# Chains of VectorE issued in turns, and two products moved ahead, in a gated attention and expert kernel

## The chip, the cores and the metric

One core of a Trainium2 chip runs the kernel. The metric is device time in microseconds. The kernel before takes 648.89 us (median of three runs, 648.76 to 652.68). The engines have their own queues and meet through semaphores: TensorE (PE, with its weight loads PEld), VectorE (DVE), ScalarE (ACT), GpSimd (POOL) and SyncE (SP), which issues transfers. An engine works through its queue in order: an instruction that waits holds up all that stand behind it.

## The reference

The input has 32 sequences of 128 tokens and 256 features. A gated attention over a context of the same shape comes first, then a layer of eight experts of which each token takes two.

```python
ig = (gi @ igate_w.T + igate_b).transpose(0, 2, 1)       # gi = [q, k, v], q = layernorm(x), k = v = ctx
fg = (gi @ fgate_w.T + fgate_b).transpose(0, 2, 1)
cs = jnp.cumsum(jax.nn.log_sigmoid(fg), axis=-1)
log_D = where(tril, cs[..., :, None] - cs[..., None, :], -inf) + ig[..., None, :]
max_log_D = jnp.max(log_D, axis=-1, keepdims=True)
C = (einsum('bhsd,bhtd->bhst', qh, kh) / sqrt(dh)) * jnp.exp(log_D - max_log_D)
normalizer = jnp.maximum(jnp.abs(C.sum(-1, keepdims=True)), jnp.exp(-max_log_D))
h = jnp.einsum('bhst,bhtd->bhsd', C / (normalizer + EPS), vh)
x = x + layernorm_per_head(h) * out_w                     # x1
xf = layernorm(x); scores = softmax(xf @ gate_w); two best experts per token
x = x + sum over the two of score * (gelu(xf @ w1[e] + b1[e]) @ w2[e] + b2[e])
```

## The kernel before

The kernel has two stages. The first goes through the sequences in eight steps of four (S0 to S7). It also loads the experts' weights and splits them into a high and a low half. The second goes through tiles of up to 256 rows that belong to one expert each.

The first stage is software-pipelined. After a prologue there are five bodies, and each works on four steps at once: `after` is the next x to come (its layer norm, its turn to features by tokens, its gates), `nxt` has its decays and its first two products made, `step` has its last two products made and its heads finished (normalizer, variance, scaling, `out_w`, x1), and `last` is routed (x1's norm `xf`, logits, choice of two experts, rows to the expert table). The last body has no `after`. The order on each engine is written out by hand in the four functions `body(last, step, nxt, after)`.

The pieces that the steps below speak of, with their lines before the change:

- VectorE: `c_of` (L1749) multiplies scores by decays, the product c of one sequence j = 0 to 3. `next_stats` (L1637 to 1643) and `next_norm` (L1631 to 1656) make the scale and shift of the next x, the last of it `minus_mean_rstd`. `next_a` (L1687, 1690) makes the gate columns, `running_max` (L1699, 1700) their running maximum, `split` three bf16 parts of it, `max_log_decay` (L1727) a sum with the turned maximum. `weights_low` (L1740) is a "weights rest", of which a body has four. `h_norm` (L1759 to 1769) makes the variance of the heads, `h_scaled` and `h_weighted` (L1780, 1785) scale them. `choose` (L1817 to 1832) is the choice of experts, eleven small instructions, and `records` what is written of it. `Chain.link` lets an instruction signal a semaphore and the next wait for it, since the next reads what it wrote.
- ScalarE: `next_guess`, `h_guess`, `x1_guess` (L720, 721) are two table lookups each that give a first guess of a reciprocal root, which Newton's step on VectorE refines. `next_normed` (L732) normalizes a sequence of the next x, `turned` (L750) copies its turn out of PSUM, `q_low` what is left, `x1_normed` (L742) makes a row block of xf, `xf_turned` and `xf_low` (L828, 760) copy its turn, `weights_high` (L801) the weights' high half, `h_out` (L809, 810) copies a sequence's heads, `decay` (L789) takes the exponential.
- TensorE: `turn` (L1142, 1145) turns a sequence of the next x, `turn_a` (L1201) the gate columns, `turn_max` (L1207) the maximum. `times_v` (L1278) multiplies c by v. `logits` (L1304), `ranks` and `decay_args` speak for themselves. `stream` (L1228) are products that nothing reads. The first `turn` of a body also waits for the fourth product, whose scores lay in the same PSUM banks.

Of the kernel before, what the change touches and what calls it, by code (L numbers as in the profile page):

```python
# [5 lines left out]
ALU = mybir.AluOpType  # L6
# [7 lines left out]
P = 128  # L14
# [33 lines left out]
def build(nc, x, ctx_in, igate_w, igate_b, fgate_w, fgate_b, out_w, gate_w, w1, b1, w2, b2, out):  # L48
# [51 lines left out]
    with ExitStack() as ctx:  # L100
# [320 lines left out]
        with nc.Block() as block:  # L421
# [287 lines left out]
            def _(act):  # L709
# [136 lines left out]
                def body(last, step, nxt, after):  # L846
                    if last is not None:
                        x1_normed(last, 0)
                        x1_normed(last, 1)
# [13 lines left out]
                    if step is not None:  # L863
                        h_out(step, 2)
# [8 lines left out]
                    if last is not None:  # L873
                        x1_normed(last, 3)
                    if step is not None:
                        h_out(step, 3)
                    if after is not None:
                        q_low(after, 0)
# [248 lines left out]
            def _(pe):  # L1127
# [205 lines left out]
                def body(last, step, nxt, after):  # L1333
                    if step is not None:
                        scores(step, 3)
                    if last is not None:
                        turn_xf(last, 0)
                    if nxt is not None:
                        log_f_sum(nxt)
                    if step is not None:  # L1340
                        stream_before(step, 2, 3)
                        times_v(step, 2)
                    if last is not None:
                        xf_left(last, 0)
# [6 lines left out]
                    if step is not None:  # L1351
                        times_v(step, 3)
# [274 lines left out]
            def _(dve):  # L1627
                dve.wait_ge(s_cp, 21)
                def refine(c, var, y, t):

                    c.link(dve, dve.tensor_tensor(t, y, y, ALU.mult))  # L1631
                    c.link(dve, dve.scalar_tensor_tensor(out=t, in0=t, scalar=-0.5, in1=var, op0=ALU.mult, op1=ALU.mult))
                    c.link(dve, dve.scalar_tensor_tensor(out=y, in0=t, scalar=1.5, in1=y, op0=ALU.add, op1=ALU.mult))

                def stats(c, src, parts, mean_var, var_eps, ready):
                    for j in range(SB):
                        c.inc(dve.bn_stats(parts[:, j, :], src[:, j, :]))  # L1637
                    c.wait(dve)
                    dve.sem_inc(s_held, 1)
                    for j in range(SB):  # L1640
                        c.inc(dve.bn_aggr(mean_var[:, j, :], parts[:, j, :]))
                    c.wait(dve)
                    dve.tensor_scalar(var_eps[:, :], mean_var[:, :, 1], LN_EPS, None, ALU.add).then_inc(ready, 1)

                def next_stats(step):
                    c_dn.begin(number(step))
                    dve.wait_ge(s_x, (number(step) + 1) * 16)
                    stats(c_dn, xin[:, :, :], st, mv, ve, s_ve)
                    c_dn.end(8)

                def next_norm(step):
# [3 lines left out]
                    refine(c_dn, ve[:, :], rs[:, :], nt1[:, :])  # L1655
# [4 lines left out]
                def gate_bias(step):  # L1660
# [5 lines left out]
                    c_dg.link(dve, dve.scalar_tensor_tensor(  # L1666
                        out=gs[:, :, :, :].rearrange("p j a h -> p j (a h)"),
                        in0=ps_gate.rearrange("p j a h -> p j (a h)"), scalar=1.0 / W_SCALE, in1=bias,
                        op0=ALU.mult, op1=ALU.add))
                    dve.scalar_tensor_tensor(out=nabs[:, :, :], in0=f, scalar=-1.0, in1=f, op0=ALU.mult,  # L1670
# [10 lines left out]
                def next_a(step):  # L1681
# [5 lines left out]
                    c_dg.inc(dve.tensor_copy(csb[:, :], ps_cs))  # L1687
                    gates_i = gs[:, :, 0, :].unsqueeze(1).broadcast_to([P, 3, SB, NH])
# [14 lines left out]
                def split(step):  # L1703
# [8 lines left out]
                    c.link(dve, dve.tensor_copy(to, runs[:, :, :]))  # L1712
                    left = runs[0:2 * G, :, :]
                    c.link(dve, dve.tensor_tensor(left, left, to[0:2 * G, :, :], ALU.subtract))
                    c.link(dve, dve.tensor_copy(to[0:2 * G, :, :], left))
# [36 lines left out]
                def h_norm(step):  # L1752
# [4 lines left out]
                    dve.wait_ge(s_en, g + 1)  # L1757
                    sq = work[:, :, :].rearrange("p j (h e) -> p (j h) e", h=NH)
                    c.inc(dve.tensor_reduce(ssq[:, :], sq, AX, ALU.add))  # L1759
                    rows = Hs[:, :, :, DH]  # L1760
                    c.link(dve, dve.scalar_tensor_tensor(out=nrm[:, :, :], in0=rows, scalar=-1.0, in1=rows,
                                                         op0=ALU.mult, op1=ALU.max))
                    c.link(dve, dve.scalar_tensor_tensor(out=nrm[:, :, :], in0=en[:, step[1], :, :], scalar=HUGE,
                                                         in1=nrm[:, :, :], op0=ALU.min, op1=ALU.max))
                    n = nrm[:, :, :].rearrange("p j h -> p (j h)")
                    c.link(dve, dve.tensor_scalar(n, n, EPS, None, ALU.add))
                    c.link(dve, dve.scalar_tensor_tensor(out=hv[:, :], in0=n, scalar=LN_EPS, in1=n,
                                                         op0=ALU.mult, op1=ALU.mult))
# [4 lines left out]
                def h_scaled(step):  # L1773
# [4 lines left out]
                    refine(c, hv[:, :], hy[:, :], ht[:, :])  # L1778
# [15 lines left out]
                def x1_stats(step):  # L1794
# [3 lines left out]
                    stats(c, xres[:, :, :], st2, mv2, ve2, s_ve2)  # L1798
# [13 lines left out]
                def choose(step):  # L1812
# [4 lines left out]
                    c.link(dve, dve.tensor_reduce(m1[:, :], ps_log, AX, ALU.max))  # L1817
                    c.link(dve, dve.tensor_tensor(dl[:, :, :], ps_log, wide(m1[:, :]), ALU.subtract))
                    c.link(dve, dve.scalar_tensor_tensor(out=key[:, :, :], in0=dl[:, :, :], scalar=0.0,
# [412 lines left out]
```

## Time and profile before

| | |
|---|---|
| runs | 648.76, 648.89, 652.68 us; median 648.89 |
| the profiled execution | 651.1 us, of which the span from first to last instruction is 649.1 |
| mean granted clock of TensorE | 0.986 of 2.4 GHz |
| busy over the span | PE 611.4 us (94%), PEld 526.6, DVE 487.2 (75%), ACT 323.4 (50%), POOL 193.7 (30%) |
| first to last third product of the bodies | 104.2 to 213.75 us |
| the expert stage's first layer-1 product | 247.73 us |

A row of the timeline gives the start in us from the span's start, the duration, engine, line, operation, output and inputs, the count, and in brackets how long the engine stood before it and for whom. The difference of two starts on one engine is what the first costs there; durations are longer than that where the next instruction starts before the first has left the pipe.

### The profile page before, as it was taken

The page shows a single profiled execution, that of the slowest core. Times are in us where ns is not written, and L with a number is a line of the kernel's source. Part 1 is how long each engine was busy: PE and PEld are TensorE (multiplying, and loading weights), DVE is VectorE, ACT ScalarE, POOL GpSimd, SP SyncE. Part 2 cuts the span into 40 slices and gives each one's busy share as a digit, 9 for nine tenths or more (in the row PEclk, how much of TensorE's full clock was granted, in tenths as well). Part 3 has the DMA queues.
Part 4 walks back from the last instruction along what each step waited for, and adds up shares of the span by engine and source line. Part 5 has one row for each costly group of instructions (what it writes and reads, how often), then busy time and mean ns, then how long its engine had stood idle before and what let it go on. Part 6 is the DMA issues. An engine that isn't in the chain of part 4 may idle for free. (4 is left out here: it accounts for less than half of the span.)

```text
span 649.1 us, 20273 instructions
## 1 busy us (share of the span) xinstructions
PE 611.4 (94%) x6736; PEld 526.6 (81%) x6737; DVE 487.2 (75%) x1330; ACT 323.4 (50%) x767; POOL 193.7 (30%) x185
## 2 busy tenths in 40 slices
PE   1799999999999899999999999999999999999995
PEld 1567777777777668998988988888989888989994
DVE  2546988999999898995888967666676757575684
ACT  2677888897988747544432323233232323232341
POOL 3000002242433424235345523232222323232333
PEclk9898998999999999999999999999999999999998
DMA  4443635475655626233464432323132323243510
GB/s 143 134 127 118 209 99 187 147 238 194 220 166 142 198 91 231 70 73 92 75 186 108 70 68 38 65 36 65 33 62 33 66 33 66 67 119 81 141 34 2
DMA packets 56044, 70.22 MB, mean 108 GB/s; under 512 B 5584, under 2 KB 50832, under 8 KB 55840
## 3 DMA queue, kind: packets, MB, share of 16 engines
q1 hardware_dynamic: 42560, 51.80, 26.3%
q0 software_dynamic: 13296, 17.32, 14.7%
q8 instruction: 49, 0.80, 0.5%
q14 instruction: 27, 0.22, 0.1%
q10 hardware_dynamic: 112, 0.08, 0.0%
HBM read 41.50 MB, written 24.92 MB: 102 GB/s over the span
## 5 line engine op out<-in xcount | busy, mean ns | idle before, releaser
L1059 ACT ACTIVATE decay_slots<-scores,b_turned 128x256 f32<-128x256 f32 (+1 forms) x312 | 124.4, 451 | 241.2 <-PE scores L1545 235.1
L1545 PE MATMUL scores<-x_slots,w_halves 128*128 128x256 f16 (+1 forms) x1760 | 193.7, 266 | 0.0
L1545 PEld LDWEIGHTS scores<-x_slots,w_halves 128*128 x1760 | 165.2, 98 | 17.3
L662 POOL DMA_INDIRECT expert_rows<-xf_rows,slot_i x64 | 71.9, 1124 | 211.8 <-issue 107.0
L1559 PE MATMUL pv<-w_halves,decay_slots 128*128 x864 | 97.6, 273 | 0.0
L684 POOL DMA_INDIRECT out_rows<-v_centred_and_one,row_ids x36 | 58.3, 1619 | 129.2 <-DVE v_centred_and_one L2146 95.7
L1559 PE MATMUL gate_bank<-w_halves,q_and_k_halves 128*128 x840 | 95.0, 273 | 0.0
L1559 PEld LDWEIGHTS pv<-w_halves,decay_slots 128*128 128x128 f16 x864 | 84.4, 98 | 9.7
L1559 PEld LDWEIGHTS gate_bank<-w_halves,q_and_k_halves 128*128 128x128 f16 x840 | 82.0, 98 | 9.5
L684 POOL DMA_INDIRECT out_rows<-work,row_ids x35 | 56.2, 1605 | 104.6 <-DVE work L2146 82.6
L1278 PEld LDWEIGHTS pv<-v_centred_and_one,decay_slots 128*128 128x128 f32 x512 | 63.7, 194 | 1.6
L1278 PE MATMUL pv<-v_centred_and_one,decay_slots 128*128 128x33 f32 x512 | 63.8, 260 | 0.0
L2133 DVE TENSOR_TENSOR decay_slots<-decay_slots 128x512 f16<-128x512 f32 (+1 forms) x80 | 51.2, 640 | 2.8
L2133 DVE TENSOR_TENSOR q_and_k_halves<-decay_slots,q_and_k_halves 128x512 f16<-128x512 f32 (+1 forms) x76 | 49.5, 651 | 2.6
L1740 DVE SCALAR_TENSOR_TENSOR w_halves<-weight_stage,w_halves 128x1024 f16<-128x1024 f32 x32 | 38.9, 1219 | 10.7 <-ACT w_halves L801 10.7
L789 ACT ACTIVATE decay_slots<-turn_bank 128x512 f32<-128x512 f32 x64 | 38.3, 598 | 8.6 <-PE turn_bank L1174 8.4
L1749 DVE SCALAR_TENSOR_TENSOR decay_slots<-scores,decay_slots 128x1024 f32<-128x1024 f32 x32 | 39.1, 1221 | 2.0 <-PE scores L1221 2.0
L2122 DVE CAST x_slots<-turn_bank 128x512 f16<-128x512 f32 (+1 forms) x39 | 25.1, 643 | 18.6 <-PE scores L1545 15.9
L1276 PE MATMUL pv<-minus_big_above,ident_bf 128*128 128x240 bf16 x128 | 34.8, 272 | 2.8 <-ACT work L810 1.7
L801 ACT ACTIVATE w_halves<-weight_stage 128x1024 f16<-128x1024 f32 x32 | 33.8, 1057 | 3.4 <-DMA weight_stage<-in_L_ffn_w 3.4
L2131 DVE CAST decay_slots<-decay_slots 128x512 f16<-128x512 f32 (+1 forms) x80 | 33.3, 416 | 2.0 <-ACT decay_slots L1059 2.0
L2131 DVE CAST q_and_k_halves<-decay_slots 128x512 f16<-128x512 f32 (+1 forms) x76 | 32.2, 423 | 0.1
(263 smaller groups left out, 864.5 us busy)
## 6 DMA issues: line engine op xcount, KB each, us to landing
weight_stage<-in_L_ffn_w SPq DMA_DIRECT2D x32, 512.0 KB, 4.0
x_slots<-in_x SPq DMA_DIRECT2D x16, 512.0 KB, 4.4
weight_stage<-expert_rows SPq DMA_DIRECT2D x30, 272.0 KB, 3.2
ctx_slots<-in_ctx SPq DMA_DIRECT2D x8, 512.0 KB, 6.0
out_rows<-x_slots SPq DMA_DIRECT2D x8, 512.0 KB
v_centred_and_one<-expert_rows SPq DMA_DIRECT2D x9, 272.0 KB, 3.0
expert_rows<-v_centred_and_one SPq DMA_DIRECT2D x9, 272.0 KB, 3.2
xf_rows<-w_halves SPq DMA_DIRECT2D x4, 512.0 KB, 4.1
```

The lines of the kernel that those rows point to most:

```text
L662: pool.indirect_dma_start(table, bass.IndirectOffsetOnAxis(ap=sloti[:, step[1], j, k:k + 1], axis=0), xfn[:, step[1], j, :], None, bounds_ ...
L684: pool.indirect_dma_start(out_rows, bass.IndirectOffsetOnAxis(ap=ids[:, k, b:b + 1], axis=0), yo[k][:, b, :], None, bounds_check=T - 1, oo ...
L789: act.activation(E[:, j, HG * r:HG * r + HG, :].rearrange("p c s -> p (c s)"), ps_t[:, :], ACT.Exp).then_inc(s_ee, 1)
L1059: ins = act.activation(hf[:, f * R:f * R + tr.rows(0)], ps_s[:, q, n * R:n * R + tr.rows(0)], ACT.Gelu, bias=b1T[:, bass.ds(expert, 1), f] ...
L1276: pe.matmul(ps_h[:, P + P + 16:512], ident_h[:, :], never[:, 0:120].unsqueeze(1).broadcast_to([P, 2, 120]), start=True, stop=True)
L1278: ins = pe.matmul(ps_h[:, h * (DH + 1):(h + 1) * (DH + 1)], E[:, j, k * KC + u, :], vaug[:, step[1], j, h, :], start=True, stop=True)
L1545: ins = pe.matmul(o, w, xh[:, tr.slot(0) % 2, b, k, 0:tr.rows(0)], start=(n == 0), stop=(n == 3 * KC - 1))
L1559: ins = pe.matmul(ps_y[k % 2][:, c * D:(c + 1) * D], hh[k % 2][:, a, f, c * P:(c + 1) * P], w, start=(f == 0 and n == 0 and c == 0), stop= ...
L1740: dve.scalar_tensor_tensor(out=lo, in0=stage[:, half, :], scalar=W_SCALE, in1=hi, op0=ALU.mult, op1=ALU.subtract).then_inc(s_lo, 1)
L1749: dve.scalar_tensor_tensor(out=c, in0=ps_s[:, :, 0:KC * P], scalar=QK_SCALE, in1=c, op0=ALU.mult, op1=ALU.mult).then_inc(s_cm, 1)
L2131: dve.tensor_copy(hi, src).then_inc(s_hhi, 1)
L2133: dve.tensor_tensor(lo, src, hi, ALU.subtract).then_inc(s_hh, 1)
```

## The change

All of VectorE's chains become generators. Where `link` signalled and waited at once, an instruction now signals, the generator yields, and the wait stands behind the yield. `go_on(chain)` issues one more piece of a chain; `whole(chain)` issues all that is left, and is used where nothing is interleaved (the prologue and the expert stage, whose order stays). The bodies' order is new on three engines. On VectorE, chains alternate, and the fourth product, the gate columns and a weights rest come ahead of the next x's scale. On ScalarE the x1 rows come behind the first h and decay and earlier than the next x's guess, and the fourth h comes ahead of the third normalization. On TensorE the fourth times-V stands ahead of the next x's first turn, and three fillers have become one ahead of the third and one ahead of the fourth times-V.

```diff
 ScalarE
-                    if last is not None:
-                        x1_normed(last, 0)
-                        x1_normed(last, 1)
                     if step is not None:
                         h_out(step, 1)
                         decay(step, 3, 1)
                     if last is not None:
+                        x1_normed(last, 0)
+                        x1_normed(last, 1)
+                    if nxt is not None:
+                        weights_high(nxt, 1)
+                    if last is not None:
                         x1_normed(last, 2)
-                        xf_turned(last, 0)
+                    if step is not None:
+                        h_out(step, 2)
                     if after is not None:
                         next_guess(after)
-                    if nxt is not None:
-                        weights_high(nxt, 1)
+                    if last is not None:
+                        xf_turned(last, 0)
+                        x1_normed(last, 3)
                     if after is not None:
                         next_normed(after, 0)
                         next_normed(after, 1)
                     if step is not None:
-                        h_out(step, 2)
+                        h_out(step, 3)
...
 TensorE
                         scores(step, 3)
+                    if nxt is not None:
+                        log_f_sum(nxt)
+                    if step is not None:
+                        stream_before(step, 2, 1)
+                        times_v(step, 2)
                     if last is not None:
                         turn_xf(last, 0)
-                    if nxt is not None:
-                        log_f_sum(nxt)
                     if step is not None:
-                        stream_before(step, 2, 3)
-                        times_v(step, 2)
+                        stream_before(step, 3, 1)
+                        times_v(step, 3)
...
 VectorE
+                def go_on(chain):
+                    next(chain, None)
+                def whole(chain):
+                    for _ in chain:
+                        pass
                 def refine(c, var, y, t):
-                    c.link(dve, dve.tensor_tensor(t, y, y, ALU.mult))
+                    c.inc(dve.tensor_tensor(t, y, y, ALU.mult))
+                    yield
+                    c.wait(dve)
...
+                    if step is not None:
+                        c_of(step, 2)
                     if last is not None:
                         x1_norm(last)
-                    if step is not None:
-                        c_of(step, 2)
-                    if after is not None:
-                        next_stats(after)
-                    if nxt is not None:
-                        weights_low(nxt, 0)
-                    if after is not None:
-                        next_norm(after)
+                    for _ in range(SB):
+                        go_on(incoming)
                     if step is not None:
                         c_of(step, 3)
-                    if nxt is not None:
-                        next_a(nxt)
+                    go_on(incoming)
+                    go_on(incoming)
+                    if nxt is not None:
+                        weights_low(nxt, 0)
+                    go_on(scaling)
+                    go_on(sums)
...
```

VectorE from the fourth product's neighbourhood to the running maximum. `bn_parts`, `mean_var`, `newton`, `rstd` and `minus_mean_rstd` belong to the next x, `log_f_sum` and `i_minus_sum` are the gate columns, L1749 and L1775 the product, L1740 and L1766 a weights rest. Before:

```order
L1641 BN_AGGR mean_var<-bn_parts 128x2 x4
L1643 TENSOR_SCALAR var_eps<-mean_var 128x4
L1740 SCALAR_TENSOR_TENSOR w_halves<-weight_stage,w_halves 128x1024
L1631 TENSOR_TENSOR newton<-rstd 128x4
L1632 SCALAR_TENSOR_TENSOR newton<-newton,var_eps 128x4
L1633 SCALAR_TENSOR_TENSOR rstd<-newton,rstd 128x4
L1656 SCALAR_TENSOR_TENSOR minus_mean_rstd<-mean_var,rstd 128x4
L1749 SCALAR_TENSOR_TENSOR decay_slots<-scores,decay_slots 128x1024
L1687 COPY log_f_sum<-gate_bank 128x32
L1690 TENSOR_TENSOR i_minus_sum<-gates,gate_bank 128x96
L1740 SCALAR_TENSOR_TENSOR w_halves<-weight_stage,w_halves 128x1024
L1699 COPY a_and_running_max<-gate_bank 96x128
```

And now:

```order
L1775 SCALAR_TENSOR_TENSOR decay_slots<-scores,decay_slots 128x1024
L1657 BN_AGGR mean_var<-bn_parts 128x2 x4
L1660 TENSOR_SCALAR var_eps<-mean_var 128x4
L1766 SCALAR_TENSOR_TENSOR w_halves<-weight_stage,w_halves 128x1024
L1640 TENSOR_TENSOR newton<-rstd 128x4
L1706 COPY log_f_sum<-gate_bank 128x32
L1643 SCALAR_TENSOR_TENSOR newton<-newton,var_eps 128x4
L1710 TENSOR_TENSOR i_minus_sum<-gates,gate_bank 128x96
L1646 SCALAR_TENSOR_TENSOR rstd<-newton,rstd 128x4
L1766 SCALAR_TENSOR_TENSOR w_halves<-weight_stage,w_halves 128x1024
L1673 SCALAR_TENSOR_TENSOR minus_mean_rstd<-mean_var,rstd 128x4
L1719 COPY a_and_running_max<-gate_bank 96x128
```

The fourth product, the gate columns and the second weights rest stood between the scale and the running maximum; now all three stand ahead of the scale, and the running maximum follows it at once.

VectorE from the sum with the turned maximum (`max_log_d`) to the scaling of the heads. `square_sum`, `normalizer` and `h_var` lead to the heads' variance, `h_newton` and `h_rstd` refine its root, `top`, `routing_work`, `xf_rows` and `chosen` are the choice. Before:

```order
L1727 TENSOR_TENSOR max_log_d<-log_f_sum,gate_bank 128x32
L1759 TENSOR_REDUCE square_sum<-work 128x32
L1761 SCALAR_TENSOR_TENSOR normalizer<-h_slots 128x32
L1763 SCALAR_TENSOR_TENSOR normalizer<-exp_minus_max,normalizer 128x32
L1766 TENSOR_SCALAR normalizer<-normalizer 128x32
L1767 SCALAR_TENSOR_TENSOR h_var<-normalizer 128x32
L1769 SCALAR_TENSOR_TENSOR h_var<-square_sum,h_var 128x32
L1740 SCALAR_TENSOR_TENSOR w_halves<-weight_stage,w_halves 128x1024
L1631 TENSOR_TENSOR h_newton<-h_rstd 128x32
L1632 SCALAR_TENSOR_TENSOR h_newton<-h_newton,h_var 128x32
L1633 SCALAR_TENSOR_TENSOR h_rstd<-h_newton,h_rstd 128x32
L1780 TENSOR_TENSOR work<-h_slots,h_rstd 128x1024
```

And now:

```order
L1753 TENSOR_TENSOR max_log_d<-log_f_sum,gate_bank 128x32
L1801 TENSOR_REDUCE square_sum<-work 128x32
L1766 SCALAR_TENSOR_TENSOR w_halves<-weight_stage,w_halves 128x1024
L1804 SCALAR_TENSOR_TENSOR h_var<-square_sum,h_var 128x32
L1852 TENSOR_REDUCE top<-route_bank 128x4
L1855 TENSOR_TENSOR routing_work<-route_bank,top 128x32
L1640 TENSOR_TENSOR h_newton<-h_rstd 128x32
L1858 SCALAR_TENSOR_TENSOR routing_work<-routing_work,rev_index 128x32
L1643 SCALAR_TENSOR_TENSOR h_newton<-h_newton,h_var 128x32
L1863 TENSOR_REDUCE xf_rows<-routing_work 128x4
L1646 SCALAR_TENSOR_TENSOR h_rstd<-h_newton,h_rstd 128x32
L1866 TENSOR_TENSOR chosen<-routing_work,xf_rows 128x32
```

The normalizer has gone up between the pieces of the split. The variance's last instruction stands behind the weights rest, and the choice, which stood behind scaling and weighting, starts ahead of the first of Newton's steps.

## Rows read from the trace of the kernel before

**Rows 1.** The page's 40 slices of the span: TensorE's busy tenths.
```profile
PE   1799999999999899999999999999999999999995
```

**Rows 2.** Stretches between third products: us, busy us by engine, clock, DMA.
```profile
core 0: us, PE busy (x) PEld busy (x) DVE busy (x) ACT busy (x) POOL busy (x), PEclk, DMA share, GB/s
104.20:131.56 27.36, 26.15 (x356) 21.67 (x345) 24.08 (x73) 22.22 (x53) 7.90 (x9) 0.94 0.62 198
158.96:186.36 27.40, 25.88 (x376) 20.97 (x376) 25.74 (x77) 23.56 (x56) 9.45 (x9) 1.00 0.64 198
213.75:243.79 30.04, 27.73 (x358) 19.90 (x356) 27.28 (x85) 16.72 (x40) 10.38 (x9) 1.00 0.50 150
```

**Rows 3.** VectorE's timeline, one body, from its third product to the next.
```profile
158.96 1.23 DVE L1749 SCALAR_TENSOR_TENSOR decay_slots<-scores,decay_slots 128x1024 f32<-128x1024 f32 x1
160.10 1.40 DVE L1637 BATCH_NORM_STATS2 bn_parts<-x_slots 128x6 f32<-128x256 f32 x4
...
163.27 0.16 DVE L1631 TENSOR_TENSOR newton<-rstd 128x4 f32<-128x4 f32 x1
...
163.85 0.16 DVE L1656 SCALAR_TENSOR_TENSOR minus_mean_rstd<-mean_var,rstd 128x4 f32<-128x4 f32 x1
163.93 1.23 DVE L1749 SCALAR_TENSOR_TENSOR decay_slots<-scores,decay_slots 128x1024 f32<-128x1024 f32 x1
...
165.33 1.22 DVE L1740 SCALAR_TENSOR_TENSOR w_halves<-weight_stage,w_halves 128x1024 f16<-128x1024 f32 x1
166.47 0.28 DVE L1699 COPY a_and_running_max<-gate_bank 96x128 f32<-96x128 f32 x1
...
171.24 0.19 DVE L1769 SCALAR_TENSOR_TENSOR h_var<-square_sum,h_var 128x32 f32<-128x32 f32 x1
...
175.56 0.18 DVE L1817 TENSOR_REDUCE top<-route_bank 128x4 f32<-128x32 f32 x1
175.78 0.19 DVE L1818 TENSOR_TENSOR routing_work<-route_bank,top 128x32 f32<-128x32 f32 x1
...
177.79 0.19 DVE L1832 TENSOR_TENSOR chosen<-routing_work,key_max 128x32 bf16<-128x32 f32 x1
177.91 0.22 DVE L1666 SCALAR_TENSOR_TENSOR gates<-gate_bank,gate_bias_rows 128x64 f32<-128x64 f32 x1
...
186.36 1.23 DVE L1749 SCALAR_TENSOR_TENSOR decay_slots<-scores,decay_slots 128x1024 f32<-128x1024 f32 x1
```

**Rows 4.** ScalarE's timeline in the same body.
```profile
157.66 0.21 ACT L720 ACTIVATE ln_var_x<-var_eps_x 128x4 f32<-128x4 f32 x1 [0.41 <-DVE var_eps_x L1643]
...
162.26 0.20 ACT L720 ACTIVATE ln_var<-var_eps 128x4 f32<-128x4 f32 x1
...
164.05 1.09 ACT L732 ACTIVATE x_slots<-x_slots,minus_mean_rstd,rstd 128x256 f32<-128x256 f32 x2 [0.41 <-DVE minus_mean_rstd L1656]
...
167.04 1.08 ACT L750 ACTIVATE q_and_k_halves<-scores 128x512 f16<-128x512 f32 x2
...
169.97 1.10 ACT L801 ACTIVATE w_halves<-weight_stage 128x1024 f16<-128x1024 f32 x1
...
171.87 0.29 ACT L720 ACTIVATE square_sum<-h_var 128x32 f32<-128x32 f32 x1
...
173.29 0.60 ACT L760 ACTIVATE xf_halves_turned<-route_bank 128x512 f16<-128x512 f32 x1
```

**Rows 5.** TensorE's timeline in the same body.
```profile
165.30 0.41 PE L1142 MATMUL scores<-ident,x_slots 128*128 128x128 f32 x2 [1.05 <-DVE decay_slots L1749]
...
165.77 0.27 PE L1201 MATMUL gate_bank<-ident,i_minus_sum 128*96 128x128 f32 x1
...
174.08 0.75 PE L1304 MATMUL route_bank<-router_w_halves,xf_halves_turned 128*128 128x8 f16 x24
```

**Rows 6.** TensorE's timeline where the expert stage begins.
```profile
247.26 0.63 PE L1525 MATMUL turn_bank<-ident,weight_stage 128*128 128x128 f32 x4
```

**Rows 7.** TensorE's timeline in the first body.
```profile
109.05 0.66 PE L1142 MATMUL scores<-ident,x_slots 128*128 128x128 f32 x2 [1.21 <-DMA ctx_slots<-in_ctx]
```

**Rows 8.** A stretch around that wait; columns as in rows 2.
```profile
108.85:112.25 3.40, 3.20 (x17) 3.15 (x17) 3.01 (x8) 3.37 (x8) 1.09 (x2) 0.50 0.62 157
```

More of the change, by code:

```diff
@@ L1832, in choose @@
+                    yield
+                    c.wait(dve)
                     dve.tensor_tensor(chosen[:, 1, :, :], key[:, :, :], wide(kmax[:, :]), ALU.is_equal).then_inc(s_mk, 1)
@@ L1916, in body @@
                 def body(last, step, nxt, after):
+                    nothing = iter(())
+                    incoming, scaling = (next_stats(after), next_norm(after)) if after is not None else (nothing,) * 2
+                    sums, bias = (next_a(nxt) if nxt is not None else nothing,
+                                  gate_bias(after) if after is not None else nothing)
+                    parted = split(nxt) if nxt is not None else nothing
+                    norm, scaled = (h_norm(step), h_scaled(step)) if step is not None else (nothing,) * 2
@@ L1917, in body @@
+                    choice, record = (choose(last), records(last)) if last is not None else (nothing,) * 2
+                    outgoing = x1_stats(step) if step is not None else nothing
+                    if step is not None:
+                        c_of(step, 2)
                     if last is not None:
                         x1_norm(last)
+                    for _ in range(SB):
+                        go_on(incoming)
                     if step is not None:
-                        c_of(step, 2)
@@ L1929, in body @@
+                    go_on(scaling)
+                    go_on(sums)
+                    go_on(scaling)
                     if nxt is not None:
-                        next_a(nxt)
                         weights_low(nxt, 1)
+                    go_on(scaling)
+                    if nxt is not None:
                         running_max(nxt)
-                        split(nxt)
+                    go_on(parted)
+                    go_on(norm)
+                    go_on(parted)
+                    go_on(norm)
@@ L1934, in body @@
+                    go_on(parted)
+                    go_on(norm)
+                    go_on(parted)
+                    go_on(norm)
+                    if nxt is not None:
                         max_log_decay(nxt)
-                    if step is not None:
-                        h_norm(step)
+                    go_on(norm)
                     if nxt is not None:
                         weights_low(nxt, 2)
+                    go_on(norm)
+                    go_on(choice)
+                    go_on(choice)
@@ L1939, in body @@
+                    go_on(scaled)
+                    go_on(choice)
+                    go_on(scaled)
+                    go_on(choice)
+                    go_on(scaled)
+                    go_on(choice)
+                    go_on(scaled)
+                    go_on(choice)
                     if step is not None:
-                        h_scaled(step)
                         h_weighted(step)
-                    if last is not None:
-                        choose(last)
-                    if after is not None:
-                        gate_bias(after)
+                    go_on(choice)
@@ L1958, in body @@
                         c_of(nxt, 2)
-                    if step is not None:
-                        x1_stats(step)
-                    if last is not None:
-                        records(last)
+                    go_on(outgoing)
+                    go_on(record)
+                    go_on(outgoing)
+                    go_on(record)
+                    go_on(outgoing)
+                    go_on(record)
+                    go_on(outgoing)
+                    go_on(record)
+                    go_on(outgoing)
+                    go_on(outgoing)
                 def first_steps():
-                    next_stats(S0)
-                    next_norm(S0)
+                    whole(next_stats(S0))
+                    whole(next_norm(S0))
                     weights_low(S0, 0)
@@ L2027, in first_steps @@
                     log_f(S3)
-                    records(S0)
+                    whole(records(S0))
                 first_steps()
```

194 lines of the change are left out of this document (120 added, 74 removed).

## The prediction

> **What bounds the kernel now.** I read the busy shares in slices first, then the stretches of single bodies, then VectorE's, ScalarE's and TensorE's timelines in one of them. After the first third of the span TensorE is full in every slice [rows 1]: the expert stage follows at its own pace, and a microsecond won or lost in the bodies ahead of it moves the end by one. The reader should see in the stretches [rows 2] that a body takes 27.40 us from one third product to the next, that TensorE is busy for 25.88 of it and VectorE's sum is 25.74; and on VectorE's timeline [rows 3] that its instructions touch one another over the whole body. So VectorE sets the 27.40. Its small instructions show two prices: a choice that needs the one in front starts 0.22 after it (175.56 to 175.78), and one that needs nothing starts 0.11 to 0.12 after it (177.79 to 177.91). That difference is what the change is after.
>
> **What it saves.** I count, in the old order, 27 places where a small instruction waits for the one in front and now has another chain's between them: 3 in Newton's steps of the next x, 3 in the split, 4 in the normalizer, 4 in the heads' scaling, 9 in the choice, 1 in the gates, 3 in the records. 27 x 0.115 = 3.1 us. The x's statistics wait some 0.2 before their sums, and the fourth product now fills that. The heads' row sum and the running maximum's column sum lose short old waits, some 0.6. Together about 3.9 us a body.
>
> **What it moves, and what then waits.** I follow one body from the third product's start, old times by [rows 3 to 5] less 158.96.
>
> First, the next x's scale (`minus_mean_rstd`). Old: 4.89 (163.85), ahead of the fourth product. Now ahead of it stand the third product (1.14, as 158.96 to 160.10), x1's scale 0.1, four statistics 1.3, the fourth product 1.14 (its slot lay behind the scale), sums 0.5 and a weights rest 1.14 (all the long ones have this slot): 5.3. Newton's first step needs ScalarE's guess. ScalarE began that at 3.30 (162.26). Now x1's guess (0.35, 157.66 to 158.01) and a decay (0.5) fall inside the stretch, since the statistics that feed the guess end last; a weights copy (1.0, as the 1.10 of 169.97) and the third h (0.5) come ahead, one turned copy (0.5) goes behind, and the fourth decay waits some 0.3 for its argument: 3.30 + 0.85 + 1.0 + 0.3 = 5.45, and the guess is there after two lookups, at 5.9. So VectorE stands 0.5. Then Newton's three steps and the two gate columns, 0.5, and another weights rest, 1.14 (165.33 to 166.47), which has also been put ahead of the scale: the scale starts at 7.6, not 4.89.
>
> Second, the running maximum. ScalarE normalizes from 7.8; its first row takes 0.6, TensorE's turn of x 0.47 (165.30 to 165.77), and the turn of the gate columns, which stands behind it on TensorE, 0.27. VectorE is at the running maximum at 7.7 and can go on at 9.2: it stands 1.5. In the old order the fourth product and a weights rest lay in between, and the columns were turned 0.7 before they were wanted (165.77 against 166.47). The change of TensorE's order doesn't help here: it put the fourth times-V ahead, into the old 1.05 wait for the fourth product [rows 5], but x's turn is now late for x.
>
> Third, the weights rest and the heads' variance. From the first normalization to the first turned copy ScalarE has the same six pieces as before, 2.99 (164.05 to 167.04): 10.8, not 8.08. The old 2.93 from there to the third weights copy (169.97) loses an x1 row and an h, 1.0, and gains 0.3 of waits for TensorE, which stands 2 us until the first turned copy is there: copy at 13.0, done at 14.05. The old order had the heads' variance (171.24) ahead of this weights rest; now it is behind, so it waits for this copy. VectorE stands 0.4 at the maximum's column sum and 0.9 at the weights rest, and the variance starts at 15.2, not 12.28. ScalarE's guess for it, in order ahead of two turned copies and x's low half, moves from 12.91 (171.87) to 15.45.
>
> Fourth, the choice. The low half came 1.42 after the guess (171.87 to 173.29), the logits 0.8 after that (174.08), and took 0.75. Now the low half starts at 16.8, the logits end at 18.15. In the old order the choice came behind the heads' scaling and weighting, 175.56, long after its logits. Now its first instruction is ahead of both, VectorE gets there at 15.3 and stands 2.9, with 2.4 us of long work queued behind that needs no logits.
>
> From the choice to the next third product the old order took 10.80 (175.56 to 186.36). Scaling and weighting move in, +3.1 (171.24 to 175.56 is 4.32, less the variance's 0.11 and one long slot), and some 20 of the 27 links go, -2.3: 11.6. So the body ends at 18.2 + 11.6 = 29.8. The other way round it's 27.40 - 3.9 + (0.5 + 1.5 + 0.4 + 0.9 + 2.9) = 29.7. I take +2.4 a body.
>
> **The sum.** Three of the four bodies with an x to come: 7.2. The first starts with its decay on the way, +1.9. The last has no x to come, but its columns' turn now stands behind the fourth times-V, its choice still waits for the logits, and the fourth product has no statistics ahead of it to cover its decay; against some 18 links saved (2.1), I take +1.6 of a range from 0 to 3, up to the second turn of rows at 247.26 [rows 6], which was 33.5 after 213.75. 10.7 in all.
>
> One more term: the clock. TensorE stood 1.21 us at 109.05 for the context rows [rows 7], and just before it went on, its granted clock fell to 0.50, the lower of its two levels (1.2 GHz), for 3.4 us [rows 8]; behind waits of 1.05 us (as at 165.30) it stayed at 1.00. The wait of 2 us for the first turned copy is longer than either. The body with the 1.21 us wait still took 27.36 [rows 2], for VectorE was the bound; now TensorE is on the path there. The cost is between 0 (absorbed, as there) and 1.7 a body (3.4 us of work at half speed), 7 in all. I take 2, nearer the row that absorbed it, since the turned copies behind have their own wait.
>
> 10.7 + 2 = 12.7. The profiled execution took 651.1 us, which gives 663.8; the median is 648.89, 2.2 below, and gives 661.6. I say 662.
>
> **The rivals.** *The waits don't bind* (10%): then VectorE's 27.40 - 3.9 = 23.5 is under TensorE, whose 25.88 less one filler of 0.2 sets a body: -1.7 x 4 and -1 in the last, 641. For it speaks that VectorE is the bound and ScalarE has 3.8 us to spare in a body (27.40 - 23.56). It decides at the scale: it would have to start by about 6, so that the columns come with VectorE.
>
> *Saved equals lost* (16%): only the first three waits bind (3.3) and the choice finds its logits, because the x1 rows, which are now done earlier, carry ScalarE's low half forward: 27.40 - 3.9 + 3.3, or -0.6 to +0.6 a body, 646 to 652.
>
> *Nothing is saved* (2%): chains in turns could be as slow as in a row. The instruction pairs in [rows 3] at 0.22 and 0.11 speak against it. The waits come on top of 27.40 then: about +6 a body, 675. The Trainium skill, "VectorE: DVE Perf Modes", section "The DRAIN you can't avoid", has such a rule: the next instruction starts only when the pipe is empty, and semaphores between chained instructions cost nothing extra. By that rule the saved 3.1 would be 0; the trace disagrees, with its 0.11 against 0.22.
>
> The forecast has 72%: 655 to 669, from a smaller fourth wait and no clock loss to half of the clock's upper bound. The range over the cases is 648 to 669, which leaves out the fast rival, some of the break-even and the far end of the clock. A measurement here can tell 1%, 6.5 us: faster 0.10, same 0.16, slower 0.74.
>
> **What would show it.** Right: a body of 29 to 31 us between third products; VectorE idle some 6 us of it, with the running maximum released by the turned columns, the weights rest by ScalarE's copy, and the choice by the logits, the longest; its small instructions 0.11 to 0.12 apart in pairs; ScalarE idle 1 us ahead of x's normalization; TensorE's idle time before the first x remainder about 2 us, with the clock at 0.50 behind some of them. Wrong: VectorE still without gaps and a body below 27; or waits at other places, above all a choice that doesn't wait.

## The result, and the profile after

The changed kernel takes 663.64 us (median of 4; 662.26 to 664.60) against 650.7 before (median of 4): a ratio of 1.0204, 95% interval [1.0159, 1.0248], so it is slower, by 1.6 to 2.5%. The forecast was 662. The profiled execution took 663.01 us, its span is 661.0. Here and below a median is over all executions of a kernel, while a ratio and its interval leave out the few that ran in the chip's slow state.

The 40 slices of TensorE's busy tenths are no longer full where the bodies lie:

```profile
PE   2799998989898989999999999999999999999995
```

The stretches of bodies, each from the start of a third product to the next, in the columns of [rows 2]: the first, a middle one, the last.

```profile
100.26:131.16 30.90, 28.04 (x380) 22.34 (x379) 23.60 (x77) 23.31 (x53) 8.77 (x9) 0.94 0.57 177
162.13:193.06 30.93, 27.67 (x376) 21.84 (x375) 23.74 (x76) 23.90 (x56) 8.10 (x9) 0.94 0.54 174
224.05:251.26 27.21, 23.37 (x296) 16.02 (x295) 21.60 (x65) 15.97 (x38) 9.63 (x9) 1.00 0.45 153
```

The middle row compares with the middle one of [rows 2]. The other two rows there are cut differently: the first begins 1.65 us behind its third product, and the last runs on to a fourth product. From third product to third product the last body took, before:

```profile
213.75:239.08 25.33, 23.02 (x295) 16.03 (x294) 22.91 (x64) 15.05 (x35) 10.38 (x9) 1.00 0.51 158
```

In the middle body VectorE's work fell from 25.74 us [rows 2] to 23.74, and the body grew by 3.5: VectorE is now idle for 7.2 us of it, where it was idle for 1.7. Where, its timeline of the middle body says (it answers to [rows 3]; in brackets the idle time and what ended it):

```profile
162.13 1.23 DVE L1775 SCALAR_TENSOR_TENSOR decay_slots<-scores,decay_slots 128x1024 f32<-128x1024 f32 x1
...
168.05 0.16 DVE L1640 TENSOR_TENSOR newton<-rstd 128x4 f32<-128x4 f32 x1 [0.40 <-ACT rstd L721]
...
169.71 0.15 DVE L1673 SCALAR_TENSOR_TENSOR minus_mean_rstd<-mean_var,rstd 128x4 f32<-128x4 f32 x1
171.35 0.29 DVE L1719 COPY a_and_running_max<-gate_bank 96x128 f32<-96x128 f32 x1 [1.49 <-PE gate_bank L1200]
...
174.28 0.19 DVE L1753 TENSOR_TENSOR max_log_d<-log_f_sum,gate_bank 128x32 f32<-128x32 f32 x1 [0.38 <-PE gate_bank L1206]
...
176.90 1.22 DVE L1766 SCALAR_TENSOR_TENSOR w_halves<-weight_stage,w_halves 128x1024 f16<-128x1024 f32 x1 [1.30 <-ACT w_halves L801]
178.04 0.18 DVE L1804 SCALAR_TENSOR_TENSOR h_var<-square_sum,h_var 128x32 f32<-128x32 f32 x1
181.50 0.19 DVE L1852 TENSOR_REDUCE top<-route_bank 128x4 f32<-128x32 f32 x1 [3.28 <-PE route_bank L1303]
181.73 0.19 DVE L1855 TENSOR_TENSOR routing_work<-route_bank,top 128x32 f32<-128x32 f32 x1
181.83 0.18 DVE L1640 TENSOR_TENSOR h_newton<-h_rstd 128x32 f32<-128x32 f32 x1
181.95 0.19 DVE L1858 SCALAR_TENSOR_TENSOR routing_work<-routing_work,rev_index 128x32 f32<-128x32 f32 x1
...
193.06 1.22 DVE L1775 SCALAR_TENSOR_TENSOR decay_slots<-scores,decay_slots 128x1024 f32<-128x1024 f32 x1
```

There are five waits, 6.9 us in all and the longest ahead of the choice, and small instructions in turns start 0.10 to 0.12 apart, where a dependent pair stood 0.22 apart [rows 3]. ScalarE in the same body, answering to [rows 4]:

```profile
167.57 0.21 ACT L720 ACTIVATE ln_var<-var_eps 128x4 f32<-128x4 f32 x1
...
169.89 1.09 ACT L732 ACTIVATE x_slots<-x_slots,minus_mean_rstd,rstd 128x256 f32<-128x256 f32 x2 [0.91 <-DVE minus_mean_rstd L1673]
...
172.89 1.07 ACT L750 ACTIVATE q_and_k_halves<-scores 128x512 f16<-128x512 f32 x2
...
175.82 1.05 ACT L801 ACTIVATE w_halves<-weight_stage 128x1024 f16<-128x1024 f32 x1
...
179.75 0.60 ACT L760 ACTIVATE xf_halves_turned<-route_bank 128x512 f16<-128x512 f32 x1
```

And TensorE, answering to [rows 5]: the first turn of x, the columns' turn, the first x remainder, the logits.

```profile
170.55 0.44 PE L1141 MATMUL scores<-ident,x_slots 128*128 128x128 f32 x2 [0.29 <-ACT x_slots L732]
...
171.04 0.27 PE L1200 MATMUL gate_bank<-ident,i_minus_sum 128*96 128x128 f32 x1
...
173.53 0.47 PE L1150 MATMUL scores<-q_and_k_halves,minus_ident_f 128*128 128x512 f16 x1 [1.78 <-ACT q_and_k_halves L750]
...
180.72 0.75 PE L1303 MATMUL route_bank<-router_w_halves,xf_halves_turned 128*128 128x8 f16 x24
```

Behind the 1.78 us wait the granted clock is at 0.50, the lower level of 1.2 GHz, in all four bodies with an x to come (columns: TensorE busy, clock, DMA share, GB/s):

```profile
173.70:177.12 3.42, 3.42 (x14) 0.50 0.70 244
```

### The profile page after: what moved, and what is told of

It is laid out like the page before. It is cut to its first block and busy times, and to the rows that moved or that the text cites. A ratio compares the mean times of both kernels' runs of the same rounds, so it can differ in the third digit from the quotient of the medians.

```text
span 661.0 us, 20263 instructions
## 1 busy us (share of the span) xinstructions
PE 616.1 (93%) x6731; PEld 528.1 (80%) x6732; DVE 476.8 (72%) x1330; ACT 325.1 (49%) x767; POOL 189.7 (29%) x185
## 5 line engine op out<-in xcount | busy, mean ns | idle before, releaser
L662 POOL DMA_INDIRECT expert_rows<-xf_rows,slot_i x64 | 68.8, 1075 | 230.5 <-issue 108.0
L1766 DVE SCALAR_TENSOR_TENSOR w_halves<-weight_stage,w_halves 128x1024 f16<-128x1024 f32 x32 | 38.9, 1219 | 14.4 <-ACT w_halves L801 14.3
L1775 DVE SCALAR_TENSOR_TENSOR decay_slots<-scores,decay_slots 128x1024 f32<-128x1024 f32 x32 | 39.0, 1220 | 3.5 <-PE scores L1220 2.0
L1166 PE MATMUL turn_bank<-pick_head,three_parts 96*128 96x512 bf16 x64 | 26.0, 406 | 7.2 <-ACT decay_slots L789 4.3
```

The lines of the kernel that those rows point to most:

```text
L662: pool.indirect_dma_start(table, bass.IndirectOffsetOnAxis(ap=sloti[:, step[1], j, k:k + 1], axis=0), xfn[:, step[1], j, :], None, bounds_ ...
L1766: dve.scalar_tensor_tensor(out=lo, in0=stage[:, half, :], scalar=W_SCALE, in1=hi, op0=ALU.mult, op1=ALU.subtract).then_inc(s_lo, 1)
L1775: dve.scalar_tensor_tensor(out=c, in0=ps_s[:, :, 0:KC * P], scalar=QK_SCALE, in1=c, op0=ALU.mult, op1=ALU.mult).then_inc(s_cm, 1)
```

## The experiments

Single executions of one kernel spread over some 9 us with the number of low clock stretches they meet (before: 646.09 us at a mean clock of 0.992, 655.29 at 0.982), so effects under 1% are read from the bodies of the profiled executions, and the totals stand beside them.

**1. x's scale ahead of the second weights rest** (the changed kernel otherwise).

```diff
                     go_on(scaling)
+                    go_on(scaling)
                     if nxt is not None:
                         weights_low(nxt, 1)
-                    go_on(scaling)
```

> The changed kernel, with one instruction moved: x's scale ahead of the second weights rest. If x's scale is the root of the waits behind it, ScalarE's normalization comes 1 us sooner and with it the turn, the copies and the logits: 0.8 us a body less, 659 to 660.5 in all. If the waits have causes of their own (the choice, the weights rest behind ScalarE's copy): no change, 663 to 664.

Measured: 656.72 us (10 runs), ratio to before 1.0096 [1.0060, 1.0131], below the changed kernel's interval; bodies 29.10 to 29.18. VectorE's wait for the columns is 0.87 instead of 1.49, and

```profile
170.19 0.39 PE L1150 MATMUL scores<-q_and_k_halves,minus_ident_f 128*128 128x512 f16 x1 [1.51 <-ACT q_and_k_halves L750]
```

TensorE's is 1.51 instead of 1.78, with no low clock in any body. So the one small instruction is worth 1.8 us a body (30.95 to 29.14), half of all that a steady body lost. I had expected 0.8; the rest is the clock, which the next run prices.

**2. Fillers in TensorE's wait**, run twice.

```diff
                     if after is not None:
+                        stream_between(nxt, 7)
                         q_left(after, 0)
```

> The changed kernel, with 7 filler products (0.22 us each) in TensorE's 1.8 us wait ahead of the first x remainder; they feed nothing. If the clock at 0.50 behind that wait is on the path, it stays at 1.00 and a body takes 29.8 instead of 30.95: 658 to 660 in all. If it is hidden, as the prediction's lower bound had it: 663 to 664.

> The kernel with fillers in TensorE's wait once more, one look: its profiled execution took 657.6 us with no low clock in the bodies, its timed ones 661 to 668. If the fillers hold the clock: again 29.8 us a body and no low stretch there, and any difference in all lies ahead of the bodies. If that was chance: low stretches in the bodies, 30.5 to 31 where they lie.

Measured in the first profiled execution: bodies of 29.78 to 29.97 with an x to come, none with a low clock, 1.02 to 1.12 less than without the fillers.

```profile
158.76:188.62 29.86, 28.11 (x383) 21.52 (x382) 23.65 (x76) 23.92 (x56) 8.18 (x9) 1.00 0.57 179
```

The second run took 666.88 us. It has the same bodies (29.54 to 29.99, clock 1.00), but a low stretch from 221.5 to 242.0 in the last body, which has none of these fillers and took 33.08; I had expected any difference ahead of the bodies. So the fillers do hold the clock where they are, and the low stretch is worth 1.0 to 1.1 us a body. Run 1's bodies, also at full clock, are 0.7 shorter than these: that is what the scale's place is worth without the clock. In all, the kernel gained nothing that can be told: 662.71 us (6 runs), 1.0207 [1.0157, 1.0256]; why low stretches come elsewhere stays open.

**3. The choice put back** behind the heads' scaling and weighting, and x1's sum with it ahead of the first product.

```diff
-                    go_on(choice)
-                    go_on(choice)
                     go_on(scaled)
-                    go_on(choice)
                     ...
                     if step is not None:
                         h_weighted(step)
+                    go_on(choice)
+                    if step is not None:
+                        x1_of(step)
+                    go_on(choice)
                     go_on(bias)
                     ...
```

> The changed kernel, with the choice put back behind the heads' scaling and weighting and then taken in turns with the gates' bias and x1's statistics, as in the run before this. If the choice's place is what costs its 3.3 us wait, as the prediction's sum has it: a body of 28 us, 651 to 654 in all. If the logits are late anyway, because x's scale is, and what follows them is just as long: the wait moves to the gates and is 0.4 a body shorter in all, 661 to 663.

Measured: 658.34 us, ratio 1.0118 [1.0074, 1.0162]; the first body 29.04, the others with an x to come 29.9 to 30.2. The 3.28 us wait is gone, and others have grown behind the same late x:

```profile
161.53 1.22 DVE L1775 SCALAR_TENSOR_TENSOR decay_slots<-scores,decay_slots 128x1024 f32<-128x1024 f32 x1 [0.42 <-ACT decay_slots L789]
...
174.89 0.19 DVE L1640 TENSOR_TENSOR h_newton<-h_rstd 128x32 f32<-128x32 f32 x1 [0.56 <-ACT h_rstd L721]
...
178.32 0.19 DVE L1852 TENSOR_REDUCE top<-route_bank 128x4 f32<-128x32 f32 x1 [0.27 <-PE route_bank L1303]
...
180.74 0.22 DVE L1683 SCALAR_TENSOR_TENSOR gates<-gate_bank,gate_bias_rows 128x64 f32<-128x64 f32 x1 [1.00 <-PE gate_bank L1186]
```

Of 3.28 us, 0.8 to 1.1 comes back in each body after the first, and 1.9 in the first. The total lies between the two expectations and nearer the second. The wait that shows longest was mostly not the choice's own price.

**4. Half of the change at a time.** VectorE's new order with the old TensorE and ScalarE orders (a), and the reverse with whole chains (b).

```diff
 (a) TensorE and ScalarE
-                        stream_before(step, 2, 1)
+                        stream_before(step, 2, 3)
 ...
 (b) VectorE
-                    go_on(scaling)
-                    go_on(sums)
+                    whole(next_norm(after))
 ...
```

> VectorE's new order alone; TensorE's and ScalarE's orders are those of before. If the late scale of x is what costs, it costs here too, and more, since the third h and x1's rows then stand in their old places: a body of 31.5 to 33 us, 664 to 671 in all. If the new orders of TensorE and ScalarE were the harm and VectorE's turns the gain: a body under 27.4, below 650.

> The other half: TensorE's and ScalarE's new orders, with VectorE's order and whole chains of before. If the new orders only fit VectorE's early fourth product: TensorE has x's first turn behind a times-V whose product VectorE makes after x's scale, so x's turn and the choice of the gates' columns come late; a body of 29.6 with the clock held, 32 with it lost, 658 to 668 in all. If the two orders are free, since ScalarE has 3.8 us to spare and TensorE the same work: 27.4, 650 to 652.

Measured: (a) 675.14 us, 1.0377 [1.0318, 1.0435], bodies 33.84 to 34.14; (b) 667.17 us, 1.0239 [1.0180, 1.0298], bodies 30.92 to 34.36. (a) is slower than the whole change and beyond what I expected; (b) lies at the upper end of what I expected, and its interval overlaps that of the whole change. Part of both is the clock: its mean over a middle body is 0.85 in (a) and 0.89 to 0.94 in (b). In (a) VectorE's normalizer, now early, waits for the last h, which ScalarE still makes late:

```profile
177.95 0.29 DVE L1719 COPY a_and_running_max<-gate_bank 96x128 f32<-96x128 f32 x1 [2.05 <-PE gate_bank L1201]
...
183.13 0.22 DVE L1785 SCALAR_TENSOR_TENSOR normalizer<-h_slots 128x32 f32<-128x32 f32 x1 [4.24 <-ACT work L810]
```

In (b) TensorE's fourth times-V stands 1.96 us for its product, with x's turn queued behind it, and VectorE then waits for the columns:

```profile
175.11 0.26 PE L1275 MATMUL pv<-minus_big_above,ident_bf 128*128 128x240 bf16 x1 [1.96 <-DVE decay_slots L1775]
...
179.37 0.29 DVE L1719 COPY a_and_running_max<-gate_bank 96x128 f32<-96x128 f32 x1 [3.00 <-PE gate_bank L1200]
```

So neither half is harmless alone.

**5. Turns without the moves.** TensorE's and ScalarE's orders of before, VectorE's places of before up to the heads' weighting; then the choice in turns with x1's sum and statistics and the gates' bias (the second run keeps the old tail in the last body):

```diff
-                    if last is not None:
-                        choose(last)
-                    if after is not None:
-                        gate_bias(after)
+                    go_on(choice)
+                    if step is not None:
+                        x1_of(step)
+                    go_on(choice)
+                    go_on(bias)
+                    ...
+                    if nxt is not None:
+                        c_of(nxt, 0)
+                    go_on(outgoing)
+                    go_on(choice)
+                    ...
```

> TensorE's and ScalarE's orders and VectorE's places are those of before; only at the end of a body are VectorE's chains taken in turns: the choice with the gates' bias and x1's statistics (x1's sum moves ahead of the first product), the heads' row sum moves behind the normalizer. If a link is worth its 0.115 us and nothing else moves, some 11 links and the statistics' 0.2 us go: a body of 26.0 us instead of 27.40, where TensorE's 25.9 takes over, and 644 to 646 us in all. If turns save nothing (the pipe is empty before each instruction anyhow): 27.4 a body, 650 to 651. If turns by themselves are what slowed the changed kernel: above 653.

> The kernel with turns at the end of the body alone (TensorE, ScalarE and VectorE's places as before), with the last body put back to its old tail, where x1's statistics lie behind the early list. The last body should go from 26.95 back to 25.3, the others stay at 26.1 to 26.5: 1.6 us less than with turns in all bodies, 643 to 646. If the last body's length was no loss (its statistics then missing later): no change.

Measured: 647.09 us, 0.9954 [0.9918, 0.9991], bodies 26.13 to 26.50 and a last one of 26.95; with the old last tail 646.85, 0.9940 [0.9908, 0.9972], last body 26.11. Both kernels are faster than the kernel before, by some 0.5%; run 7 tells whether that is the turns or x1's earlier sum. The repair gave 0.84 us in the last body instead of 1.6, too little to show in the total.

**6. Without the fillers** of the old order, on the kernel of 5.

```diff
-                        stream_before(step, 2, 3)
+                        stream_before(step, 2, 0 if after is not None else 3)
...
-                        stream_between(nxt, 1)
+                        stream_between(nxt, 0 if after is not None else 1)
```

> The run beside it, without the four filler products (0.22 us each) of a body. If TensorE's 25.8 is the bound there: 25.0 to 25.4 a body, where VectorE takes over again, 3 us less, 640 to 643. If the fillers hold the clock through TensorE's waits: low stretches of 3.4 us come back behind those waits and each costs up to 1.7: 645 to 650.

Measured: 653.0 us, 1.0039 [1.0002, 1.0076]: 6 us slower than with them. An undisturbed body stays at 26.14, so TensorE's 25.8 was not the bound; VectorE, which waits for others in only 0.5 us of that body, is. And two of the bodies (27.71 and 28.18) lose their clock behind a wait for the context rows; the wait and body of the second, with the undisturbed body below it:

```profile
162.98 0.66 PE L1142 MATMUL scores<-ident,x_slots 128*128 128x128 f32 x2 [1.48 <-DMA ctx_slots<-in_ctx]
```

```profile
156.06:184.24 28.18, 26.48 (x373) 22.04 (x372) 24.90 (x77) 23.86 (x57) 9.54 (x9) 0.94 0.59 191
184.24:210.38 26.14, 24.94 (x373) 20.55 (x372) 24.72 (x77) 23.64 (x57) 9.26 (x9) 1.00 0.58 185
```

**7. The links alone, and the context rows.** The kernel of 5 with the same places but whole chains; then both with the context rows loaded earlier on SP's queue.

```diff
+                    if after is not None:
+                        load_ctx(after)
                     if nxt is not None:
                         weights(nxt, 1)
                     if last is not None:
                         write_x1(last)
-                    if after is not None:
-                        load_ctx(after)
```

> The best kernel so far, with the same pieces in the same part of the body (x1's sum ahead of the first product, the row sum behind the normalizer) but each chain whole: choice, gates' bias and x1's statistics one behind another. If the gain is the links (11 of 0.115 us and the statistics' 0.2 us), it is gone: 27.2 to 27.5 us a body, 649 to 651 in all. If the gain is x1's sum being earlier: 26.1 a body stays, 645 to 648.

> The best kernel so far (turns at the end of the body, old last body), with one line moved on SP's queue: the context rows are loaded ahead of the second weights and of x1's write, which wait for VectorE's last weights rest, instead of behind them. [...] If they are only late by chance, or the load then takes the rings from the weights: no change, 646 to 648.

> The same line moved in the kernel whose chains are whole. If its long bodies (32 to 34 us) were the context rows' wait and the clock lost behind it: 27.2 to 27.8 a body, 649 to 651 in all, and what is left against the run beside it, 1.1 to 1.6 us a body, is the price of the links alone. If the chains themselves cost that much: 32 to 34 us stay, 654 or more.

Measured: whole chains 654.76 us, 1.0055 [1.0018, 1.0092], slower than I expected; with early context rows 647.05, 0.9976 [0.9951, 1.0001], so the excess was theirs. Chains in turns with early context rows: **642.86 us, 0.9916 [0.9882, 0.9950]**, just under the 643 to 645.5 that I expected if TensorE's wait for those rows counted. It is the lowest median here, ahead of both kernels; but its interval overlaps that of the kernel with the old last tail (run 5), so the totals do not show what the early rows are worth there. The pair with early context rows, whole and in turns:

```profile
157.70:185.06 27.36, 25.87 (x376) 20.95 (x376) 25.70 (x76) 23.64 (x57) 10.07 (x9) 1.00 0.67 197
```

```profile
151.06:177.21 26.15, 25.82 (x377) 20.96 (x376) 24.84 (x77) 23.64 (x57) 8.69 (x9) 1.00 0.69 206
```

Only the order within this part of the body differs, so turns are worth 1.21 us there: 11 links and the statistics' 0.2 us, or 0.09 a link. With whole chains a body is as long as in the kernel before (27.36 against 27.40), so x1's earlier sum alone gives nothing. In the trace of whole chains the choice's instructions start 0.21 to 0.23 apart; in turns:

```profile
169.54 0.18 DVE L1858 SCALAR_TENSOR_TENSOR routing_work<-routing_work,rev_index 128x32 f32<-128x32 f32 x1
169.66 0.19 DVE L1689 SCALAR_TENSOR_TENSOR minus_abs_f<-gates 128x32 f32<-128x32 f32 x1
169.77 0.18 DVE L1863 TENSOR_REDUCE xf_rows<-routing_work 128x4 f32<-128x32 f32 x1
169.86 1.21 DVE L1775 SCALAR_TENSOR_TENSOR decay_slots<-scores,decay_slots 128x1024 f32<-128x1024 f32 x1
```

## Why the prediction was right, and where it was not

**The waits: right, one by one.** Times from the third product's start, forecast and then measured in the body from 162.13. Newton's wait 0.5: 0.40. The scale at 7.6: 7.58. ScalarE's normalization at 7.8 after 1 us idle: 7.76 after 0.91. The running maximum at 9.2 after 1.5: 9.22 after 1.49. The maximum's column sum 0.4: 0.38. The turned copies at 10.8: 10.76. TensorE's wait of 2: 1.78. Up to here nothing is off by more than 0.22. From 11.6 on the clock is low, and all is late: the weights copy at 13.0 came at 13.69, the weights rest waited 1.30 and not 0.9, the variance 15.91 and not 15.2, the choice 19.37 and not 18.2, after 3.28 and not 2.9. From the choice to the next third product 11.6 was forecast and 11.56 measured. With the clock held by fillers (run 2) the weights rest waits 0.84, the choice 2.83, and a body takes 29.86: the forecast's 29.8. One slip helped: the forecast's own pieces put the end of the logits at 16.87 + 0.79 + 0.75 = 18.4, not 18.15, which would make a body of 30.0; with the clock held the choice came at 18.30.

**The clock: undersized.** This is the term of the sum that was mis-sized. The forecast took 2 us in all, near its lower end of 0, since the old first body had a low stretch and "still took 27.36". That row misled me. The stretch in [rows 2] begins at 104.20, but the third product of that body began at 102.55:

```profile
102.55:131.56 29.01, 27.72 (x380) 22.75 (x379) 25.73 (x76) 23.78 (x56) 8.54 (x9) 0.94 0.60 193
```

The body took 29.01, 1.6 more than its neighbours. Nothing was absorbed; what the row had shown was a price near the upper bound of 1.7. Measured in the changed kernel, against the bodies with fillers: 1.0 to 1.1 in each of four bodies, 4.3 in all. The upper end of the forecast's main case does not follow from its reason either: 648.89 + 10.7 and half of the clock's 7 make 663, not 669.

**The sum came out by two more accidents.** Against before, the middle bodies grew by 3.57, 3.53 and 3.60: 10.7, where 7.2 and most of the clock's 2 were forecast. The first grew by 1.89, as forecast, but it is the 2.4 of the others and 1.1 of its own clock, less the 1.6 that the old first body had lost to the same thing. The last grew by 1.88; up to the second turn of rows, the forecast's mark, it is 1.73 for a forecast of 1.6, and by the end 1.6. That makes 14.2. Ahead of the bodies 2.29 came back. The older execution had a low stretch there,

```profile
50.82:54.23 3.41, 3.41 (x23) 2.21 (x15) 0.36 (x3) 2.72 (x6) 0.00 (x0) 0.50 0.04 13
```

and the later one has none, so most of this is chance and no part of the change; 0.26 of it lies right ahead of the first third product, where the change has moved small instructions. What is left is the span's 11.9. So the waits and the clock made the kernel slower as foreseen, but that 662 was met so closely is luck.

**The savings** were real but a little smaller: 0.09 a link and not 0.115 (run 7). In the middle body the five waits make 6.9 and the growth is 3.5, so some 3.3 was saved, where 3.9 was forecast. The Trainium skill, "VectorE: DVE Perf Modes", section "The DRAIN you can't avoid", says that a semaphore between chained instructions costs nothing extra. By that the pair of run 7 would have been equal; 27.36 against 26.15 disagrees. The same section adds, and the prediction does not say it, that a next instruction that is not held starts earlier; the starts 0.09 to 0.12 apart in run 7 agree with that.

**The choice's 2.9** was the right wait at the place, but not the choice's price: put back, it returns about 1.0 of 3.28 a body (run 3). The logits were late because x's scale was: with the scale one slot of 1.14 us earlier and the clock at 1.00 in both, the choice starts 17.54 us behind the third product of a middle body (run 1) instead of 18.30 (run 2). That slot was worth 1.8 a body, 0.7 of it without the clock. What the other delays ahead of the scale (the early fourth product, the sums, ScalarE's pieces in front of the guess) cost each was not tried alone.

## What to carry to other kernels

Take dependent chains in turns with their neighbours where they stand, and move nothing that another engine waits for: here the turns are worth 1.2 us a body, and the change that brought them with x's scale 2.7 us later cost 3.5. In a row of waits, the longest can be where the lateness ends up and not where it starts, as here; follow it back to the first instruction that came later than it used to. And measure a repeated body from the same instruction to the same instruction, or a loss hides in the cut.

## What the runs showed that I had not expected

The length of TensorE's wait did not decide whether its clock fell. Behind 1.51 us (run 1) the clock stayed at 1.00 in every body; behind 1.48 (run 6) it stayed in one body, shown here, and fell in the next:

```profile
136.34 0.41 PE L1142 MATMUL scores<-ident,x_slots 128*128 128x128 f32 x2 [1.48 <-DMA ctx_slots<-in_ctx]
```

```profile
129.41:156.06 26.65, 24.94 (x373) 20.56 (x372) 24.70 (x77) 23.76 (x57) 8.87 (x9) 1.00 0.59 202
```

And in the first body of run 7's whole chains with early context rows it fell behind 1.02, where the kernel in turns kept it behind 1.03 at the same place:

```profile
107.75 0.66 PE L1142 MATMUL scores<-ident,x_slots 128*128 128x128 f32 x2 [1.02 <-DVE decay_slots L1775]
```

```profile
101.41:130.33 28.92, 27.05 (x372) 22.07 (x372) 25.68 (x76) 23.52 (x56) 9.86 (x9) 0.94 0.60 185
```

What else decides is open. The low stretch cost 1.0 to 1.1 us in the changed kernel, 1.5 in run 6 (28.18 against 26.65) and 1.6 in that first body (28.92 against 27.36).

A kernel whose bodies got 1.3 us shorter met the next limit at once. In run 5's second kernel the context rows land 6.2 to 6.4 us after an issue that stands behind a wait for VectorE's last weights rest; in two of the four bodies that is 0.3 and 0.8 us after TensorE wants them. Issued ahead of that wait (run 7), they are never waited for.
